# Softmax maxima turned by a trip through DRAM in place of TensorE, and expert down products in three reduced-precision passes

## The reference

```
x = x + L0_xattn(layernorm(x), ctx)      # softmax(q k / sqrt(8)) v, 16 heads, 256 queries x 256 keys
x = x + L0_ffn(layernorm(x))             # W_exp, 9 butterfly stages, gelu, 9 butterfly stages, W_con
x = x + L1_xattn(layernorm(x), ctx)
x = x + L1_ffn(layernorm(x))             # router: sigmoid, top 4 of 16, weights c_e
#   y = sum_e c_e * (silu(x w13_gate_e) * (x w13_up_e)) w2_e  +  shared expert
```

## Time and profile before

| | us |
|---|---|
| median of three runs | 209.72 (208.79 to 210.5) |
| the profiled execution | 209.94 |
| its span in the trace | 207.8 |
| PE busy / DVE / ACT / POOL | 197.7 / 154.2 / 146.7 / 55.6 |

### The profile page before, as it was taken

The page is one execution under the profiler, slowest core; times in us unless marked ns, Lnnn a source line. Parts: engine busy times, 40 slices in busy tenths (PEclk is TensorE's granted clock), DMA queues, the critical chain, the costliest instruction groups (busy, mean ns, idle before and its releaser), DMA issues.

```text
span 207.8 us, 4287 instructions
## 1 busy us (share of the span) xinstructions
PE 197.7 (95%) x1727; PEld 110.7 (53%) x1727; DVE 154.2 (74%) x243; ACT 146.7 (71%) x262; POOL 55.6 (27%) x72
## 2 busy tenths in 40 slices
PE   7798899999999999997999999999999999999993
PEld 4464367564574543443344566554566745766640
DVE  0399989899998764259975989999775664795482
ACT  2865873989886999972795998987999936613230
POOL 7948940039046000059000000040000252300400
PEclk9999999999999999999999999999999999999999
DMA  6950000000004400000000000000000352003641
GB/s 177 323 224 3 0 0 5 2 3 0 3 0 131 197 3 0 0 5 0 0 0 3 0 5 0 3 0 3 0 5 6 122 205 80 0 6 136 179 142 50
DMA packets 5795, 10.50 MB, mean 51 GB/s; under 512 B 1120, under 2 KB 2576, under 8 KB 5648
## 3 DMA queue, kind: packets, MB, share of 16 engines
q1 hardware_dynamic: 4208, 6.16, 9.3%
q0 software_dynamic: 848, 3.53, 4.5%
q10 hardware_dynamic: 720, 0.53, 0.9%
HBM read 9.64 MB, written 0.59 MB: 49 GB/s over the span
## 4 chain that ended last, share of the span: by engine, by line
PE 81%; DVE 7%; ACT 4%; DMA 2%; issue 2%; SPq 1%; POOL 1%
PE PS L363 60%; PE OB L363 21%; DVE T L1003 3%; DMA spread<-comb_out 2%; SPq L658 1%; DVE attn L1033 1%; DMA comb_out<-comb_t 1%; DVE k_lo L940 1%; DVE xn L991 1%; ACT K L830 1%; POOL hid_t L777 1%; ACT sq L853 1%; ACT sq L856 1%; ACT sq L840 0%; DVE x L1047 0%
## 5 line engine op out<-in xcount | busy, mean ns | idle before, releaser
L1003 DVE TENSOR_REDUCE T<-PS 128x4 f32<-128x1024 f32 x64 | 76.6, 1220 | 4.8 <-PE PS L363 4.2
L864 ACT ACTIVATE P<-PS 128x512 f32<-128x512 f32 x128 | 68.1, 603 | 14.0 <-PE PS L363 13.3
L363 PE MATMUL OB<-P,V 128*32 128x256 f32 x512 | 33.4, 384 | 0.1
L363 PE MATMUL PS<-K,Q 32*128 32x256 f32 x256 | 28.2, 323 | 0.5 <-ACT sq L856 0.3
L363 PEld LDWEIGHTS PS<-K,Q 32*128 32x128 f32 x256 | 17.6, 183 | 17.0 <-ACT P L864 6.9
L363 PE MATMUL PS<-Q,K 32*128 32x256 f32 x256 | 25.6, 320 | 0.3
L363 PEld LDWEIGHTS PS<-Q,K 32*128 32x128 f32 x256 | 16.4, 183 | 11.5 <-ACT P L864 5.1
L777 POOL TENSOR_TENSOR hid_t<-spread,prod_t 128x512 f32<-128x512 f32 x7 | 9.3, 1325 | 46.6 <-DMA spread<-comb_out 37.3
L917 ACT ACTIVATE gate_t<-PS 128x512 f32<-128x512 f32 (+1 forms) x18 | 10.3, 596 | 16.1 <-DVE prod_t L1112 12.0
L363 PEld LDWEIGHTS OB<-P,V 128*32 128x32 f32 x512 | 14.3, 109 | 10.6 <-ACT P L864 0.9
L765 POOL TENSOR_TENSOR attn<-o_raw,sums 128x512 f32<-128x512 f32 x4 | 5.1, 1282 | 44.9 <-ACT sums L883 44.8
(11 more groups left out here) (125 smaller groups left out, 324.8 us busy)
## 6 DMA issues: line engine op xcount, KB each, us to landing
spread<-comb_out SPq DMA_DIRECT2D x32, 128.0 KB, 3.0
w_gu<-gu POOLq DMA_DIRECT2D x1, 1024.0 KB, 5.5
w<-w2p POOLq DMA_DIRECT2D x1, 512.0 KB, 5.8
outT<-x SPq DMA_DIRECT2D x2, 256.0 KB, 2.9
e_up<-eup POOLq DMA_DIRECT2D x1, 508.0 KB, 6.1
e_dn<-edn POOLq DMA_DIRECT2D x1, 508.0 KB, 6.4
w_exp<-wexp POOLq DMA_DIRECT2D x1, 258.0 KB, 6.2
x<-xT SPq DMA_DIRECT2D x2, 128.0 KB, 3.0
```

The lines of the kernel that those rows point to most:

```text
L363: return nc.tensor.matmul(out, lhsT, rhs, start=start, stop=stop)
L864: finish(nc.scalar.activation(P[:, (JOINT * U + j) % (JOINT * PUNITS), :, :].rearrange("p k q -> p (k q)"), PS[:, FILLED["sc", U, j // 2][ ...
L1003: finish(nc.vector.tensor_reduce(dst, two("max", U, i).rearrange("p j (t s) -> p j t s", t=2), AX.X, ALU.max, negate=True), "red", U, i)
```

## The change

1. **Maxima through DRAM.** `turn`, `shift`, the zeroing of `T` and the two slots of `T` are gone. `T` has a slot for each unit. SP gets a table of its own, `SP_ORDER`, with two steps for each unit: `st.U` waits for both `red.U` and stores `T` to `turn_out` in DRAM, element by element, since neighbours in DRAM are on different partitions in `T` (128 partitions x 8 elements of 4 bytes); `ld.U` waits for that store and loads four rows of 256 elements into the spare rows of `Q`. `sc.U` waits for the load.
2. **Three passes elsewhere.** `up`, the shared expert's `gate` and the 16 `dn` of expert pairs are made in three passes. This adds the steps `uhi`, `ulo` (high and low part of the normed rows, 512 columns, for each half), `hhi`, `hlo` (the same of `hid_t` for each pair), `w2split` (POOL, splits `w_2` and `w_gus`) and one more subtraction at `fwr.3`. `dn` waits for `hlo` where it waited for `hid`.
3. **The last addition and store in halves** of 256 columns, the second one issued by ACT; one table of ACT is loaded at the start.
4. **All orders are new**, with 42 idle matmuls where there were 31, and other steps of DVE and ACT: DVE has 6 `ocopy` where it had 3 and 8 `qev` where it had 4; POOL has 6 `hid` and 7 `hlo` where it had 7 `hid`. The new tiles of the experts lie where `V` of layer 0, `cx` and `sel_in` were.

```diff
-TURNED = ((1, 1, 2),) + ((2, 2),) * 7
...
+SP_ORDER = """
+st.0 ld.0 st.1 ld.1 st.2 ld.2 st.3 ld.3 st.4 st.5 ld.4 st.6 ld.5 ld.6 st.7 ld.7 st.8 st.9 ld.8 ld.9 st.10 st.11
+ld.10 st.12 ld.11 ld.12 st.13 st.14 ld.13 st.15 ld.14 ld.15 st.16 ld.16 st.17 st.18 ld.18 ld.17 st.20 st.19
+ld.20 ld.19 st.21 st.22 ld.21 ld.22 st.23 ld.23 st.24 ld.24 st.25 ld.25 st.26 st.27 ld.26 ld.27 st.28 ld.28
+st.29 st.30 ld.29 st.31 ld.30 ld.31
 """
...
-            def turn(t):
-
-                take()
-                for U in reversed(TURN_UNITS[t]):
-                    for i in (1, 0):
-                        after(pe, "red", U, i)
...
-                for qt in range(2):
-                    for j in range(JOINT):
-                        rows = slice(32 * j, 32 * j + 32)
-                        last = mm(bank("turn", t)[rows, qt * D:(qt + 1) * D], T[:, t % TURNS, qt, rows], EYE)
-                give(last, "turn", t)
-
             def scores(U, i):
                 l, b, g = unit(U)
                 take()
-                after(pe, "shift", turned_with(U))
+                turned_waited(pe, U)
...
+            def three(to, w_high, w_low, high, low, start=True, stop=True):
+
+                mm(to, w_high, high, start=start, stop=False)
+                mm(to, w_high, low, start=False, stop=False)
+                return mm(to, w_low, high, start=False, stop=stop)
...
-                give(mm(bank("up", c, k), w_up[:, k, :], xn[:, chunk(c)]), "up", c, k)
+                give(three(bank("up", c, k), w_up_hi[:, k, :], w_up_lo[:, k, :], n_hi[:, :], n_lo[:, :]), "up", c, k)
...
                 if e < EPAIRS:
-                    after(pe, "hid", c, e)
-                    w, h = w_2[:, e, :], hid_t[:, i % 2, :]
+                    after(pe, "w2split")
+                    after(pe, "hlo", c, e)
+                    last = three(OB[:, :], w_2hi[:, e, :], w_2lo[:, e, :], hid_hi[:, i % 2, :], hid_lo[:, i % 2, :],
+                                 start=e == 0, stop=False)
...
+            def store_maxima(U):
+                for i in (1, 0):
+                    after(sp, "red", U, i)
+                if U >= RING:
+                    stored_waited(U - RING)
+                sp.dma_start(turn_out[U].rearrange("j t q -> q j t"), T[:, U, :, :].bitcast(f32),
+                             allow_slow_non_contiguous=True).then_inc(turned_out[U % RING], 16)
+
+            def load_maxima(U):
+                l, b, g = unit(U)
+                stored_waited(U)
+                if U >= RING:
+                    turned_waited(sp, U - RING)
+                sp.dma_start(Q[g:D:32, g, queries(b)].bitcast(f32).rearrange("j (t q) -> j t q", t=2),
+                             turn_out[U]).then_inc(turned_in[U % RING], 16)
...
-                dst = T[:, t % TURNS, :, :].rearrange("p t (j r) -> p j t r", r=32)[:, 2 * i:2 * i + 2, :, g]
-                finish(nc.vector.tensor_reduce(dst, two("max", U, i).rearrange("p j (t s) -> p j t s", t=2), AX.X,
+                finish(nc.vector.tensor_reduce(T[:, U, 2 * i:2 * i + 2, :], two("max", U, i).rearrange("p j (t s) -> p j t s", t=2), AX.X,
                                                ALU.max, negate=True), "red", U, i)
...
+            def low_hidden(c, e):
+                i = (EPAIRS + 1) * c + e
+                after(dve, "hhi", c, e)
+                parts_free(dve, c, e)
+                finish(nc.vector.tensor_tensor(hid_lo[:, i % 2, :], hid_t[:, i % 2, :],
+                                               hid_hi[:, i % 2, :].bitcast(f32), ALU.subtract), "hlo", c, e)
```

More of the change, by code:

```diff
@@ L30 @@
 BANKS = 7
-TURNS = 2
 PUNITS = 3
+RING = 8
 SPREADS = 4
 BQ, BK, BO, BCON, BDOWN, BUP, ONES = 0, 2, 4, 6, 7, 8, 12
-TURNED = ((1, 1, 2),) + ((2, 2),) * 7
[L40 to L43, removed]
-PE_ORDER = """
-fill.7:0 centre.0:0 kproj.0.0:1 centre.1:2 avg.0:3 kproj.0.1:4 avg.1:5 fill.1:6 qproj.0.0:6 ksel.0.0.2:0
-ksel.0.1.3:3 fill.2:1 qsel.0.0.1:1 ksel.0.0.0:4 ksel.0.1.2:6 qsel.0.0.0:5 ksel.0.1.0:2 ksel.0.0.3:3
@@ L49 @@
[L49 to L67, removed]
-qsel.1.1.2:6 qsel.1.1.3:5 sc.21.0:01 pv.19 sc.21.1:36 max.26.0:01 sc.22.0:24 pv.20 max.26.1:34 sc.22.1:05
@@ L69 @@
-sc.23.0:16 pv.21 turn.13:2 max.27.0:34 sc.23.1:05 pv.22 max.27.1:12 sc.24.0:06 pv.23 sc.24.1:35 max.28.0:12
-sc.25.0:04 fill.4:6 max.28.1:56 turn.14:3 pv.24 max.29.0:12 max.29.1:56 sc.25.1:04 out.1.0:3 sc.26.0:01
-sc.26.1:24 max.30.0:56 pv.25 turn.15:3 max.30.1:01 sc.27.0:45 centre.7:6 sc.27.1:23 max.31.0:45 avg.7:0
-max.31.1:12 sc.28.0:34 sc.28.1:56 pv.26 pv.27 turn.16:0 sc.29.0:12 sc.29.1:36 logits.0:5 gate.0.0:2 sc.30.0:04
-sc.30.1:35 pv.28 pv.29 sc.31.0:16 sc.31.1:05 gup.0.0:3 gate.0.1:4 comb.0:0 pv.30 pv.31 gate.0.2:5 gup.0.1:1
@@ L901, in high_tokens, with high_rows, high_hidden @@
                 finish(nc.scalar.activation(k_hi[:, chunk(c)], xn[:, chunk(c)], ACT.Copy), "xh", c)
+            def high_rows(c):
+                after(act, "normed", norm(1, c))
+                for v in range(NCH):
+                    filled(act, "vproj", v)
+                for p in range(len(SPANS[1])):
+                    filled(act, "kproj", 1, p)
+                if c:
+                    for k in range(BLK):
+                        filled(act, "up", c - 1, k)
+                finish(nc.scalar.activation(n_hi[:, :], xn[:, chunk(c)], ACT.Copy), "uhi", c)
+            def high_hidden(c, e):
+                i = (EPAIRS + 1) * c + e
+                after(act, "hid", c, e)
+                parts_free(act, c, e)
+                finish(nc.scalar.activation(hid_hi[:, i % 2, :], hid_t[:, i % 2, :], ACT.Copy), "hhi", c, e)
             def router_exp(c):
@@ L925, in _ @@
                 steps[name](*at)
+            for c in range(NCH):
+                after(act, "moeadd", c)
+                half = slice(c * CH + CH // 2, (c + 1) * CH)
+                act.dma_start(outT[:, half], x[:, half]).then_inc(stored_too, 16)
         @block.vector
```

289 lines of the change are left out of this document (183 added, 106 removed).

## The result

| | before | after |
|---|---|---|
| median of four, us | 209.89 (208.79 to 210.5) | 349.26 (348.14 to 352.64) |
| ratio, 95% interval | | 1.6695 [1.6607, 1.6783] |
| span of the profiled execution | 207.8 | 346.8 |
| PE busy / idle in it | 197.7 / 10.1 | 234.6 / 112.2 |
| mean granted clock of TensorE | 0.998 | 0.749 |

The forecast was 202.5. The changed kernel takes 139 us more, far outside 195 to 214. (Some executions of most kernels here, before included, fall to a lower clock by themselves; ratios leave the slow ones out.)

A forecast was written before the change was run, and what follows sets the result against it. PE's own work, busy 95% of the span, was taken to bound the kernel nearly everywhere: 209.9 - 9.4 - 4.4 + 2.4 + 1.0 + 1.5 + 2.0 - 0.3 = 202.7 us profiled, 202.5 for the median, range 195 to 214.

The forecast's parts named there:

- The trip through DRAM: Attention, from a unit's last reduce to its row in `Q`: store lands after 3.0 us, whole trip 4.8 us.
- SP keeps up: SP's in-order queue in attention: a store and load-issue round of 3.4 us fits the 4.25 us per unit.
- slow-store rival: Scattered store in attention lands after about 4.6 us or more, SP's round exceeds a unit: 210.5 to 225 us, chance 0.23.
- The covers: PE's steps between a unit's `max` and `sc` hide most of reduce plus trip, 6.0 us; remaining waits +2.0 us.
- The load: Four rows from DRAM into `Q` for each unit in attention, taken as 1.7 us by its size.
- 17 turns, -9.4 us: Attention: each turn removed from PE frees 0.55 us until the next step, counted in full, -9.4 us.
- Three passes, -4.4 us: `up`, shared gates and `dn`: three passes take 0.69 us against 0.86 plain, 26 conversions at 0.17 us, -4.4 us.
- the chains of +1.0 and +1.5: Added splitting steps lengthen dependencies: +1.0 us before `up` of half 1, +1.5 us in the experts' stage.
- Collisions of DVE and POOL: Rival in the experts' stage: shared-port collisions cost up to 1.1 us each, 207 us; collisions or longer chains, chance 0.15.
- the parts other than the trip: Whole kernel: turns -9.4, passes -4.4, idle matmuls +2.4, longer chains +1.0 and +1.5, halved last store -0.3 us.

The follow-up runs named there:

- probe: Kernel before plus 27 groups of transfers, one after another on SP's idle queue: the changed kernel's store took 9.2, 11.3, 10.5 us, the 4-row load 1.7.
- q1: Kernel before in its own orders, without the 17 turns, the 17 shifts and the scores' wait for them: 213.9 us, ratio 1.0138.
- r4: Changed kernel without its 32 stores, 32 loads and the scores' wait for them: 208.5 us, ratio 0.9885.

## Why the prediction was wrong

- **The failed step** is under "The trip through DRAM": "64 packets are 1.5 to 4.7 us, so the store lands after 3.1 to 6.3 us ... I take 3.0, nearest to the small packets." It measured 9.9 us, above both ends, and 3.0 lies even under the lower one. The bound was drawn from how long packets take, and they took 8 ns; what takes long is the completion of neighbouring 4-byte writes, which no row of before held. I named the missing row and then let the nearest one close the range. The overlap that rested on it failed with it: "SP keeps up" had a round of 3.4 us under the 4.25 of a unit, and the round was 10.3.
- **The slow-store rival** had the mechanism, SP's round over 4.25 us, and the side. Its price stopped at 225 us, with the same upper end of the landing and no clock: the 42 us by which PE's matmuls ran longer were in no term.
- **The covers.** "I take +2.0 us" for 4.8 us of trip: with 4.3 us it was 6 us. The count of PE's steps held in quiet stretches (3.1 us was free), but one load met POOL's weights. So a right price of the store wouldn't have saved the sum.
- **The load** at 1.7 us was right when alone (probe 1.7; 2.1 for the last one, 289.01 in the trace after), and not beside a store in flight or POOL's loads (8.5 and 11.15 us in the trace after).
- **17 turns, -9.4 us.** In q1 PE's busy time at a full clock fell by 6.1 us only, and waits took 3.6 and the clock 4.6 of what was to be gained. I had let a step taken off PE count in full "unless something else is late at once", from the chain's 81% PE, and counted nothing for the two engines that I called close behind; that share tells what limited before, not what comes next.
- **Three passes, -4.4 us**, and the chains of +1.0 and +1.5 that they add: PE -3.8, idle +3.4. Passes stand 0.23 us apart as forecast; the chains were 0.9 us too cheap. In the stage itself r4's PE waits for `route` (1.7 us) and `hid_lo` (0.9). Collisions of DVE and POOL are small there: no `hid` or `hlo` of DVE took over 1.02 us, where the rival had up to 1.1 us on top of 0.69.
- **Together** the parts other than the trip were to give 9.2 us and gave 2.4.

Open: why neighbouring writes are slow. 256 packed elements cost what 1024 do, which fits writes to the same 64 bytes following each other at about 10 / 16 = 0.6 us each (an estimate); no run varied how many share them. Whether another order of SP's stores and loads, or more stores in flight at once, would have hidden the landing: no run tried it. And what makes the clock fall: gaps came before, but the same gap stood once with a fall behind it and once without, and the traces don't show the rule.
